# Layer 1 experts: second product feature-major in two split parts, with the gate weights spread by DMA and multiplied into its input

## Reference, cut to what matters

```python
raw_gate = softmax(x @ gate)                       # 16 experts
gate_topk = top3(raw_gate); gate_topk /= sum(gate_topk)
hidden = relu(einsum('btd,edh->bteh', x, W1) + b1) # h = 256
expert_out = einsum('bteh,ehd->bted', hidden, W2) + b2
return einsum('bte,bted->btd', gate_topk, expert_out)
```

## Time and profile before

| what | us |
|---|---|
| median of 3 runs | 2126.52 (2126.18 to 2131.17) |
| the profiled execution, its own time | 2133.49 |
| its span | 2131.8 |
| expert stage of layer 1, first tile's turn to the last second product | 1207.9 to about 1721.1 |
| attention stage of layer 1 | about 1721 to 2131.8 |

### The profile page before, as it was taken

The page is one execution under the profiler, slowest core; times in us unless marked ns, Lnnn a source line. Parts: engine busy times, 40 slices in busy tenths (PEclk is TensorE's granted clock), DMA queues, the critical chain, the costliest instruction groups (busy, mean ns, idle before and its releaser), DMA issues. The chain is left out here.

```text
span 2131.8 us, 32693 instructions
## 1 busy us (share of the span) xinstructions
PE 1652.0 (77%) x8418; PEld 1194.2 (56%) x8418; DVE 1599.4 (75%) x4329; ACT 1133.8 (53%) x1811; POOL 1024.1 (48%) x1108
## 2 busy tenths in 40 slices
PE   3286787886868868687785599998999988778877
PEld 2163454554535545354452488887888855555554
DVE  3499999999999999999998444444444466677663
ACT  1365465564746646456453345454454556666664
POOL 2577778687786867868887100000000013233322
PEclk8598788897988979889897699999999989999997
DMA  5420020110201102002002211110110000000000
GB/s 83 105 56 1 1 66 1 31 36 1 65 1 24 42 1 65 0 12 49 1 11 68 71 26 23 25 26 9 23 23 9 26 15 16 15 15 22 15 15 13
DMA packets 140707, 58.82 MB, mean 28 GB/s; under 512 B 94743, under 2 KB 135180, under 8 KB 140556
## 3 DMA queue, kind: packets, MB, share of 16 engines
q1 hardware_dynamic: 140556, 57.19, 12.0%
HBM read 36.05 MB, written 21.10 MB: 27 GB/s over the span
## 5 line engine op out<-in xcount | busy, mean ns | idle before, releaser
L612 ACT ACTIVATE shared_rings<-pb 128x512 f32<-128x512 f32 (+1 forms) x784 | 434.7, 598 | 361.1 <-PE pb L639 318.3
L688 PE MATMUL pb<-hid,shared_down 128*128 128x512 f32 x528 | 308.8, 670 | 156.7 <-POOL hid L490 154.0
L486 POOL TENSOR_TENSOR hid<-shared_rings 128x512 f32<-128x512 f32 x256 | 334.2, 1306 | 177.3 <-ACT shared_rings L612 162.5
L490 POOL TENSOR_TENSOR hid<-hid,shared_rings 128x512 f32<-128x512 f32 x256 | 329.9, 1289 | 20.6 <-POOL hid L486 1.0
L1814 DVE SCALAR_TENSOR_TENSOR l_acc<-l_pb,l_gtok,l_acc 128x128 f32<-128x128 f32 x512 | 144.3, 344 | 255.5 <-PE l_pb L1458 255.5
L637 PE MATMUL pb<-xt_hi,shared_hi 128*128 128x512 f32 (+1 forms) x264 | 191.9, 727 | 96.6 <-ACT shared_rings L612 96.6
L1373 ACT ACTIVATE l_hid<-l_pb,l_cols 128x512 f32<-128x512 f32 x256 | 169.3, 687 | 182.9 <-PE l_pb L1458 182.6
L1458 PEld LDWEIGHTS l_pb<-l_big,l_hid 128*128 128x128 f32 x2048 | 247.1, 192 | 10.6
L1458 PE MATMUL l_pb<-l_big,l_hid 128*128 128x128 f32 x2048 | 247.9, 275 | 0.0
L1287 POOL TENSOR_TENSOR l_ql<-l_rope,l_qh 128x512 f32 x8 | 10.3, 1284 | 459.1 <-ACT l_qh L1367 459.1
L688 PEld LDWEIGHTS pb<-hid,shared_down 128*128 128x128 f32 x528 | 102.6, 209 | 214.9 <-POOL hid L490 188.1
(11 more groups left out here) (319 smaller groups left out, 3821.5 us busy)
## 6 DMA issues: line engine op xcount, KB each, us to landing
z_scratch<-zs SPq DMA_DIRECT2D x128, 81.0 KB, 3.0
zr<-z_scratch SPq DMA_DIRECT2D x8, 1296.0 KB, 8.1
x_sb<-in_L_attn_x_dram SPq DMA_DIRECT2D x32, 64.0 KB, 2.0
shared_rings<-in_L_ffn_We_gate_dram SPq DMA_DIRECT2D x4, 512.0 KB, 5.7
shared_rings<-in_L_ffn_We_up_dram SPq DMA_DIRECT2D x4, 512.0 KB, 6.7
g_scratch<-zs SPq DMA_DIRECT2D x8, 256.0 KB, 2.8
y_scratch<-yo SPq DMA_DIRECT2D x8, 256.0 KB, 2.1
shared_down<-in_L_ffn_W_dram SPq DMA_DIRECT2D x4, 512.0 KB, 6.1
```

The source lines that it names most:

```text
L486: pool.tensor_tensor(hid1[:, :], g, u, ALU.mult).then_inc(s_h1, 1)
L490: pool.tensor_tensor(hid[:, (p + par) % 2, :], hid1[:, :], c, ALU.mult).then_inc(s_h, 1)
L612: act.activation(dst, pb[0:n, what, :], ACT.Silu if what == 0 else ACT.Copy).then_inc(s_ev, 1)
L688: last = pe.matmul(pb[:, SUM, :], wd[0:n, p, :], hid[0:n, (p + par) % 2, :], start=(p == 0), stop=(p == PAIRS), skip_group_check=True)
```

## The change

1. The second product is feature-major: out[feature, token] = sum over r of W2[r]ᵀ · hidden[r], three fp32r matmuls of 512 columns for each r (w2_hi*hid_hi, w2_hi*hid_lo, w2_lo*hid_hi). All 32 r and the bias product (b2 with the transposed gate weights) accumulate in one PSUM bank (6 or 7 by the tile's parity), with start only at the bias.
2. As the gate weight now varies along the free axis, it is multiplied into the hidden rows. The transposed gate weights gT go to DRAM and come back by broadcasting DMAs, eight for a tile, each of two experts' rows to 128 partitions (512 KB), into `gates`, a ring of four pairs that takes the place of the raw W2. POOL multiplies each relu row by its gate row in place (32 multiplications of 128x512 in a tile).
3. The gated rows are split: the hi part by DVE for even r and by ACT for odd r, the lo part by DVE for all r (32 subtractions in a tile).
4. DVE's L1814 goes away, and so does the start of `acc` on ACT. silu reads the PSUM bank, PE transposes the result back to token-major (four transposes) and ACT copies it out, all during the next tile.
5. The rotary products, the turn and the routing move from the boundary to between the r; the second product runs four r behind the first (LAG = 4).
6. q and k are kept in plain fp32 (`qk`) after their gelu. They are split in the attention stage, one batch at a time: hi on ACT, lo on POOL.
7. Before tile 0, W2 is loaded in eight DMAs and split in four chunks of 128x1024, hi on ACT and lo on POOL.

Core of the diff (the routing code that is only cut into stages and the attention's loop bounds are left out):

```diff
@@ places
-        PE_AT = {1: "yT", 3: "mix", 9: "xT", 12: "router"}
-        ACT_AT = {5: "yT", 12: "square", 15: "sqrt", 20: "xT", 30: "exp"}
-        MIX_AT, CENTRE_AT, SELECT_AT = (3, 5, 6, 9), 13, (8, 10)
+        PE_AT = {0: "yT", 3: "mix", 12: "xT", 15: "router", 22: "gT"}
+        ACT_AT = {1: "yT", 6: "square", 9: "sqrt", 12: "xT", 17: "exp", 20: "kv", 22: "gT"}
+        DVE_AT = {2: "mix", 3: "centre", 6: "var", 8: "xn", 11: "xT", 14: "peak", 16: "softmax", 17: "top", 18: "gate"}
+        QK_AT, ROPE_AT, GELU_AT = (5, 8, 11, 14), (4, 7, 9, 13), (18, 19)
+        OUT_AT, SILU_AT, COPY_AT, SELECT_AT = 6, 4, 7, (22, 27)
@@ sync
+            def gate_rows(t, q, first):
+                if not first or q >= HELD:
+                    sp.wait_ge(s_mul, t * R1 + 4 * (q - HELD) + 4)
+                at = q % HELD
+                sp.dma_start(gates[:, 2 * at:2 * at + 2, :].rearrange("p q n -> p (q n)"),
+                             gT_dram[bass.ds(t, 1), 2 * q:2 * q + 2, :].rearrange("o e n -> o (e n)").to_broadcast([P, 2 * TOK])).then_inc(s_gate[at], 16)
@@ gpsimd
+            for i in range(4):
+                at = slice(i * (E1 // 4) * F1, (i + 1) * (E1 // 4) * F1)
+                pool.wait_ge(s_w2h, i + 1)
+                pool.tensor_tensor(w2_lo[:, at], big2[:, at], w2_hi[:, at].bitcast(F32), ALU.subtract).then_inc(s_w2s, 1)
             with pool.Fori(0, NT) as t:
-                (lo of q, lo of k)
+                for r in range(R1):
+                    q, e = r // 4, r // 2
+                    if r % 4 == 0:
+                        pool.wait_ge(s_gate[q % HELD], t * 32 + 16 * (q // HELD + 1))
+                    pool.wait_ge(s_hid, t * R1 + (r + 1))
+                    row = hid[:, r % HR, :]
+                    pool.tensor_tensor(row, row, gates[:, e % (2 * HELD), :], ALU.mult).then_inc(s_mul, 1)
@@ scalar
+            def hidden(t, r, first):
+                act.wait_ge(s_w1o, t * R1 + (r + 1))
+                if not first or r >= HR:
+                    act.wait_ge(s_lo, t * R1 + (r + 1 - HR))
+                act.activation(hid[:, r % HR, :], pb[:, 2 + r % 3, :], ACT.Relu, bias=cols[:, r:r + 1]).then_inc(s_hid, 1)
+            def hidden_hi(t, r, first):
+                act.wait_ge(s_mul, t * R1 + (r + 1))
+                if not first or r >= HR:
+                    act.wait_ge(s_w2o, t * R1 + (r + 1 - HR))
+                act.activation(hid_hi[:, r % HR, :], hid[:, r % HR, :], ACT.Copy).then_inc(s_hio, 1)
@@ scalar, tile: hidden(t, r), then after each even r
+                    hidden_hi(t, r - 1, first)
@@ tensor
+            def summed(t, par, r):
+                pe.wait_ge(s_lo, t * R1 + (r + 1))
+                out, at, slot = pb[:, ACC + par, :], slice(P * r, P * (r + 1)), r % HR
+                mm(out, w2_hi[:, at], hid_hi[:, slot, :], start=False, stop=False)
+                mm(out, w2_hi[:, at], hid_lo[:, slot, :], start=False, stop=False)
+                mm(out, w2_lo[:, at], hid_hi[:, slot, :], start=False, stop=(r == R1 - 1)).then_inc(s_w2o, 1)
@@ vector
-                    dve.wait_ge(s_w2o, t * E1 + (e + 1))
-                    for s in range(NS):
-                        dve.scalar_tensor_tensor(out=acc[:, s, :], in0=pb[:, 5 + e % 2, sub], scalar=gtok[par][:, s, e:e + 1], in1=acc[:, s, :], op0=ALU.mult, op1=ALU.add)
+            def hidden_parts(t, r, first):
+                slot = r % HR
+                if r % 2 == 0:
+                    dve.wait_ge(s_mul, t * R1 + (r + 1))
+                    if not first or r >= HR:
+                        dve.wait_ge(s_w2o, t * R1 + (r + 1 - HR))
+                    dve.tensor_copy(hid_hi[:, slot, :], hid[:, slot, :]).then_inc(s_hie, 1)
+                    dve.wait_ge(s_hie, t * E1 + (r // 2 + 1))
+                else:
+                    dve.wait_ge(s_hio, t * E1 + (r // 2 + 1))
+                dve.tensor_tensor(hid_lo[:, slot, :], hid[:, slot, :], hid_hi[:, slot, :].bitcast(F32), ALU.subtract).then_inc(s_lo, 1)
```

More of the change, by code:

```diff
@@ new lines, in sp_tile @@
+            def sp_tile(t, first, ahead, load):
+                gate_rows(t, HELD, first)
+                if ahead:
+                    keep_x2(t + 1)
+                gate_rows(t, HELD + 1, first)
+                if not first:
+                    keep_gate(t - 1)
+                if load:
+                    next_inputs(t + 2)
+                for q in range(HELD + 2, 2 * HELD):
+                    gate_rows(t, q, first)
+                if ahead:
+                    keep_gT(t + 1)
+                    for q in range(HELD):
+                        gate_rows(t + 1, q, False)
@@ L1377, in _ @@
-            for stage in ("yT", "square", "sqrt", "xT", "exp"):
+                    hidden(t, r, first)
+                    if r % 2 == 0 and r:
+                        hidden_hi(t, r - 1, first)
+                    elif r == 0 and not first:
+                        hidden_hi(t - 1, R1 - 1, False)
+            front(0, 0, "yT")
+            for i in range(4):
+                at = slice(i * (E1 // 4) * F1, (i + 1) * (E1 // 4) * F1)
+                act.wait_ge(s_w2[i], 32)
+                act.activation(w2_hi[:, at], big2[:, at], ACT.Copy).then_inc(s_w2h, 1)
@@ L1386, in a_unit @@
+            tile(NT - 1, 1, False, False)
+            hidden_hi(NT - 1, R1 - 1, False)
+            silu(NT - 1, 1)
+            gate_out(NT - 1, 1)
             def a_unit(b, par, i):
@@ L1544, in _, with hidden @@
-            for stage in PE_AT.values():
+                else:
+                    pe.wait_ge(s_gt, t + 1)
+                    for s in range(NS):
+                        last = pe.transpose(pb[0:E1, 1, sub[s]], gtok[par][:, s, :], ident[:, :])
+                    last.then_inc(s_gT_ps, 1)
+            def hidden(t, par, r, first):
+                if r < 2 and not first:
+                    pe.wait_ge(s_hid, t * R1 + (r - 1))
+                elif r >= 3:
+                    pe.wait_ge(s_hid, t * R1 + (r - 2))
+                at = slice(P * r, P * (r + 1))
+                split3(pb[:, 2 + r % 3, :], w1_hi[:, at], w1_lo[:, at], xt[par][:, 0, :], xt[par][:, 1, :]).then_inc(s_w1o, 1)
@@ L1553, in a_unit @@
+            for r in range(R1 - LAG, R1):
+                summed(NT - 1, 1, r)
+            gate_out(NT - 1, 1)
             def a_unit(b, par, i):
@@ new lines, in tile @@
+            def tile(t, par, first, ahead):
+                for r in range(R1):
+                    if first and r == 0:
+                        for stage in ("softmax", "top", "gate"):
+                            front(0, 0, stage)
+                    if ahead and r in DVE_AT:
+                        front(t + 1, 1 - par, DVE_AT[r])
+                    if r in ROPE_AT:
+                        turn(t, ROPE_AT.index(r))
+                    if not ahead and r in SELECT_AT:
+                        selectors(SELECT_AT.index(r))
+                    hidden_parts(t, r, first)
@@ L1927, in build @@
         layer0(nc, d, (z, y, g0), sem, area)
[L1928 removed]
+        layer1(nc, d, (y, g0, x2, g1, gT), out, sem, area)
 def constants():
```

442 lines of the change are left out of this document (238 added, 204 removed).

## The result

The changed kernel takes 2188.39 us (median of 4 runs, 2186.39 to 2194.2), the kernel before 2126.91 (4 runs, 2126.18 to 2131.17). The ratio is 1.0275, 95% interval 1.0254 to 1.0296: slower, by 61.5 us. Forecast were 2196 and a range of 2125 to 2265.

The account below looks back on a forecast made before the run. PE set the expert stage before, at 65.2 us a tile; after, POOL and DVE excluding each other would, at 71. +60 by that stage's end, +3.5 and +5.5 in attention made +69 on the span; forecast 2196 us, range 2125 to 2265.

Parts of the forecast that it names:

- The mechanism: In the expert stage, POOL's multiplications and DVE's subtractions and casts of SBUF data exclude each other, so each waits.
- PE's side: Expert stage: twelve matmuls make 2.9 us an expert instead of 3.18; a tile set by PE would be about 56.5.
- Rival A: Expert stage: the exclusion costs little and PE still sets the pace; tile 56.5 us, time 2082; chance 0.13.
- The queue of DVE and POOL: Expert stage: operations that waited cost 0.14 us less; a pair of r takes 3.9, between 3.68 and 4.38.
- The start: Before tile 0's gating: W2's split delays the layer norm, gate weights go through DRAM; POOL's first product at about 1220.
- The transposes and the copy: At the start, gate weights are transposed and copied before going to DRAM: 1.2 us.
- The store: At the start, gate weights are stored to DRAM, with SP's wait for it: 1.7 us.
- The load: At the start, a 512 KB load brings gate rows back from DRAM: 6.7 us, taken from We_up.
- rival E: Gate-row broadcast loads are slow, binding above 9 us each; at 12 a tile is 96 us, time 2400; chance 0.03.
- Attention: After the expert stage: +3.5 us before the first product, +5.5 from 0.4 a batch over 14 batches.
- The sum: Whole kernel: +60 to the expert stage's end, +3.5 and +5.5 in attention, +69 on the span; time 2196 us.
- the tile: Expert stage: 16 pairs at 3.9 us, uncovered DVE work and 1 for ACT make 71; bounds 62.1 and 82.2.

Follow-up runs that it names:

- Experiment 2: Changed kernel with all hi parts on ACT, POOL multiplying only the first column, then clearing 1200 elements of an unused buffer: 2075.04 us.
- Experiment 3: Changed kernel with jobs re-dealt: DVE adds bias and gates from PSUM, ACT does two relus, POOL subtracts for lo: 2075.73 us, 0.9746 of before.
- Experiment 4: before_busy_pool: the kernel before plus 32 idle POOL multiplications of 128x512 a tile, both inputs in SBUF: 2131.43 us, ratio 0.9999.
- experiment 5: w2_split_late: changed kernel, POOL's split of W2 waiting for tile 0's gate weights, first gate-row loads for a quarter of the split each: 2183.16 us.
- experiments 1: Changed kernel with ACT writing every hi part and DVE only the lo parts: 2146.73 us, 1.0079 of the kernel before.
- 6: Two kernels on one chip: DVE gating from PSUM, repeated (2069.34 us), and with late W2 split and tile 0's gate weights transposed first (2064.16 us).
- gate_from_psum_again: Repeat of the changed kernel with DVE gating from PSUM, ACT doing two relus, POOL the lo subtraction: 2069.34 us, 0.9729 of before.

## Why the prediction was right

**The mechanism is shown.** Experiment 2 removes nearly all of POOL's reads and leaves its time, its waits and its place, and the subtraction falls from 1.32 to 0.69 and the time by 72 us. Experiment 3 deals the jobs out anew, so that DVE's operand comes from PSUM, and gets the same time. Experiment 4 shows that a busy POOL by itself does nothing to DVE's operations with one input in PSUM (344 ns before, 345 beside it), while one with two SBUF inputs went from 0.69 to 1.17. The Trainium skill, "SBUF — State Buffer", section "Who interferes with whom", draws the line where these runs do: two SBUF inputs on DVE against a GpSimd instruction that reads SBUF, "not with one that only writes it".

**PE's side.** Said: twelve products at about 0.24, 2.9 an expert, a PE-bound tile of 56.5. Experiment 3, where PE is full, has 55.4. Twelve matmuls take 2.80 there (1436.06 to 1438.86) at a clock of 1.00, which at the 0.97 of the kernel before would be 2.89 by an estimate: the 2.9 was right, and the rest of the tile's difference is within what the clock gives. (The terms as written, 65.2 - 4.5 - 4.5 + 0.5, make 56.7, not 56.5.) Rival A's time was 2082; experiment 3, which meets the exclusion only in a few operations, has 2076, and 2069 when taken again.

**The queue of DVE and POOL.** Said: an operation that waited ends its duration less 0.14 after the other, so 0.55 for the subtraction; the timeline has 0.54. The median subtraction of 1.64 says that more than half of them met a multiplication; of the casts some four in ten did, by an estimate from their mean of 0.87, 0.42 when free and about 1.5 when blocked. That 0.42 is also the cast's price in the prediction, where no row had it. Forecast were 71 us a tile, measured 69.9. From the first multiplication to silu the forecast had 561.5 us (7 x 71 + 63 + 1.5) and the run 553.8; 7.7 too much, 6.6 of it in the six tiles between the table loads (six times 71 against 419.4).

**The start.** Said: first multiplication at 1220, which is 28.3 us after tile 0's first DVE operation (L1711 at 1191.74 in the kernel before); measured 31.4. The delay by the split was taken as 4, and experiment 5 has 3.8 up to the gate weights. The three terms behind it were off both ways. The transposes and the copy took 4.6 instead of 1.2 (gate weights ready 1211.67, copy ended 1216.22), since PE had the next tile's transposes of y and two first products of tile 0 ahead of them (1211.10 to 1214.54); the prediction did not look at that queue. The store with SP's wait took 3.6 instead of 1.7. The load took 4.1 instead of 6.7: spread from one row of DRAM to 128 partitions, 512 KB landed no later than We_up's 512 KB, and rival E falls. The DMA row of the page after, whose last number is the median us from issue to landing:

```profile
l_big<-gT_scratch SPq DMA_DIRECT2D x64, 512.0 KB, 3.7
```

The two errors, 3.1 too short and 7.7 too long, partly cancel, which is luck: the end of the stage was forecast 60 later than before and came 55.8 later, counted from tile 0's first DVE operation (585.2 against 529.4).

**Attention.** Said: +9, of it 0.4 a batch because POOL's new subtraction holds DVE's small cast. The mechanism is there, at a smaller size, 0.25; the cast that took 0.20 in the earlier trace rows has a median of 0.45 over the 16 batches after, and the timeline at one batch's end shows it ending 0.05 after POOL's subtraction:

```profile
1915.96 1.28 POOL L1382 TENSOR_TENSOR l_w_lo<-l_qk,l_w_hi 128x512 fp32r<-128x512 f32 x1
1916.84 0.45 DVE L2006 CAST l_mhl<-l_mrow 128x32 fp32r<-128x32 f32 x1
```

From the last second product to the end the changed kernel took 414.7 us and the kernel before 410.7. But the six other executions above with the same code in this part (experiments 1, 2, 3, 5 and 6), counted from the last silu, took from 409.2 to 417.9, and the granted clock of the stretch orders them: 409.2 and 409.6 at 0.97, 412.1 at 0.96, 412.9 at 0.94, 414.9 at 0.92, 417.9 at 0.91. The changed kernel's own 414.7 is at 0.93. The windows of the kernel before and of gate_from_psum_again (the clock is the third number from the end):

```profile
1721.10:2131.80 410.70, 317.96 (x2400) 208.92 (x2399) 269.44 (x500) 260.53 (x386) 123.93 (x390) 0.94 0.06 16
1656.00:2068.90 412.90, 318.26 (x2404) 210.07 (x2404) 272.48 (x496) 269.49 (x403) 143.80 (x406) 0.94 0.06 16
```

At the same clock, 0.94, the new code takes 412.9 and the old 410.7 (and 410.2 in before_busy_pool). By this estimate, from one execution each, the term is some 2 to 3 us and not 9.

**The sum.** 2196 was 7.6 too much. The mis-sized terms are the tile (71 for 69.9, seven times) and attention (+9 for 4.0 in the profiled executions, 2 to 3 at equal clock), against a start that was 3 too short. That tile was built with guesses of what is covered (60% of 7.5 us of other DVE work, 3.9 for a pair between 3.68 and 4.38), and no run here separates these guesses from each other. The mechanism was right and the tile lay well inside its bounds; that the sum came within 8 us owes something to luck, since the start was too short where the rest was too long.

## What to carry to other kernels

Before work is moved from PE to "idle" VectorE and GpSimd, count for both the operations that excluded each other here: two SBUF inputs or a cast on VectorE, multiplications and subtractions of SBUF tiles on GpSimd. Add the durations of both engines, less a start-up per wait, and compare that one sum with the engine that sets the pace now; here the sum was estimated at 62 us a tile against PE's 56, while each engine alone was below 42. It leaves out VectorE's other work; with that the tile took 69.9. The remedy here was to re-deal the jobs so that VectorE's operand comes from PSUM: the time of the same computation went from 1.028 to 0.975 of the time before, and to 0.971 with its start mended.

## What was not expected of the hardware

In experiment 2 the clearing on POOL let a subtraction of 128x512 with two SBUF inputs through untouched, but it blocked a tiny operation with one input. From the source view:

```profile
L1918 DVE TENSOR_SCALAR l_row<-l_row x8: 170/1014/1018, 1211.0 to 1593.0; 128x4 f32<-128x4 f32 x8
```

128x4 elements took 1.01 us at the median and 0.17 at the least. The timeline shows one of them, started 0.11 after a clearing and ended 0.03 after it:

```profile
1313.44 1.10 POOL L1355 MEMSET l_pt<- 128x1200 f32 x1
1313.55 1.02 DVE L1918 TENSOR_SCALAR l_row<-l_row 128x4 f32<-128x4 f32 x1
```

In these runs, then, a GpSimd instruction that only writes excludes another set of forms than one that reads. The Trainium skill, "SBUF — State Buffer", section "Who interferes with whom", counts `tensor_scalar` and `cast` among the forms that can take both of the shared ports; the row agrees. And an ordinary small store, 32 KB of gate weights to DRAM, kept the queue for 3.6 us in the changed kernel (issue 1216.24 to the next issue 1219.86) but for 1.6 in w2_split_late (1206.31 to 1207.91); what lengthened it was not looked for.
